# Row maxima transposed in fp32, then split into two bf16 rows on the way out of PSUM

## What is computed

```
attn = einsum('bhqd,bhkd->bhqk', q, k) * scale
attn = softmax(attn)                       # exp(score - row maximum) / sum
y = einsum('bhqk,bhkd->bhqd', attn, v)
```

## Time and profile before

| what | before |
|---|---|
| runs: median (lowest to highest) | 5286.25 us (5284.78 to 5296.24), 3 runs |
| profiled execution: device time | 5298.91 us |
| its span | 5297.2 us |
| PE, DVE, ACT, POOL busy | 93%, 74%, 73%, 38% |
| stage A, first and last row copy | 139.1 to 1118.2 us |
| stage X | 1187.2 to 2217.0 us |
| stage F | 2283.1 to 3630.5 us |

### The profile page before, as it was taken

One profiled execution on the slowest core, in us unless ns is written; L12 is line 12 of the kernel. 1 busy time (PEld: TensorE's weight loads), 2 busy tenths in 40 slices (PEclk: granted clock), 3 DMA queues, 4 the chain that ended last, 5 costly groups with the idle time before them and its releaser, 6 DMA issues. The chain is left out here.

```text
span 5297.2 us, 147856 instructions
## 1 busy us (share of the span) xinstructions
PE 4926.9 (93%) x45659; PEld 4001.1 (76%) x45660; DVE 3899.7 (74%) x9253; ACT 3865.1 (73%) x8215; POOL 2027.2 (38%) x1692
## 2 busy tenths in 40 slices
PE   0999999979999999889999999995799999999998
PEld 0777777758888888667777777773599999899997
DVE  7888888868888888689999999997744444344433
ACT  5899999958888888767777777773655555555554
POOL 1222232313333333234444444442144544444443
PEclk9999999989999999999999999997799999999999
DMA  6777777746666666467777777772432332323222
GB/s 189 184 188 187 190 186 189 187 125 194 196 196 197 196 197 197 138 170 185 186 185 186 183 185 186 185 185 70 52 64 47 63 57 45 64 49 64 47 47 28
DMA packets 631700, 750.63 MB, mean 142 GB/s; under 512 B 143365, under 2 KB 560334, under 8 KB 631472
## 3 DMA queue, kind: packets, MB, share of 16 engines
q1 hardware_dynamic: 575136, 679.62, 49.0%
q0 software_dynamic: 49152, 63.09, 7.3%
q10 hardware_dynamic: 7184, 5.00, 0.3%
HBM read 476.49 MB, written 272.24 MB: 141 GB/s over the span
## 5 line engine op out<-in xcount | busy, mean ns | idle before, releaser
L1762 POOL DMA_INDIRECT out_dram<-exp_gated,exp_token x256 | 419.7, 1639 | 717.6 <-ACT exp_gated L1666 377.1
L1011 DVE TENSOR_REDUCE F_tops<-F_score 128x2 f32<-128x512 f32 x1024 | 668.8, 686 | 22.6 <-PE F_score L706 14.3
L1712 DVE TENSOR_TENSOR exp_hT_lo<-exp_whole,exp_hT_hi 128x512 fp32r<-128x512 f32 x512 | 355.4, 694 | 437.1 <-ACT exp_hT_hi L1655 437.1
L871 ACT ACTIVATE F_probs<-F_scoreT 128x512 f32<-128x512 f32 x1024 | 571.4, 591 | 74.7 <-PE F_scoreT L677 73.4
L1011 DVE TENSOR_REDUCE A_tops<-A_score 128x3 f32<-128x384 f32 x1024 | 526.9, 553 | 83.9 <-PE A_score L696 65.5
L1615 PE MATMUL exp_res<-exp_w_hi,exp_hT_hi 128*128 128x256 f32 x2048 | 573.5, 280 | 0.0
L1617 PE MATMUL exp_res<-exp_w_lo,exp_hT_hi 128*128 128x256 f32 x2048 | 568.0, 277 | 0.0
L1618 PE MATMUL exp_res<-exp_w_hi,exp_hT_lo 128*128 128x256 f32 x2048 | 567.9, 277 | 0.0
L1666 ACT ACTIVATE exp_gated<-exp_y,exp_gate 128x256 f32<-128x256 f32 x256 | 109.4, 498 | 624.1 <-DVE exp_y L1736 594.5
L871 ACT ACTIVATE A_probs<-A_scoreT 128x384 f32<-128x384 f32 x1024 | 463.3, 481 | 17.2 <-PE A_scoreT L665 8.8
L1602 PE MATMUL exp_hid<-exp_xT_hi,exp_w_lo 128*128 128x512 f32 x1024 | 405.9, 396 | 0.0
(11 more groups left out here) (355 smaller groups left out, 14326.1 us busy)
## 6 DMA issues: line engine op xcount, KB each, us to landing
QS<-d_q SPq DMA_DIRECT2D x384, 192.0 KB, 3.7
KS<-d_k SPq DMA_DIRECT2D x256, 192.0 KB, 4.0
QS<-d_q SPq DMA_DIRECT2D x384, 128.0 KB, 3.8
KS<-d_k SPq DMA_DIRECT2D x256, 128.0 KB, 4.0
d_q<-A_q_parts SPq DMA_DIRECT2D x64, 384.0 KB, 3.0
d_k<-A_k_parts SPq DMA_DIRECT2D x64, 384.0 KB, 2.8
QS<-d_q SPq DMA_DIRECT2D x384, 64.0 KB, 3.6
d_q<-X_q_parts SPq DMA_DIRECT2D x64, 384.0 KB, 2.6
```

Source lines behind the costliest of these rows:

```text
L871: nc.scalar.activation(probs[m][0:KR, at:at + HB, :].rearrange("p u x -> p (u x)"), scoreT[i % TB][0:KR, 0:HB * TCOL], ACT.Exp)\
L1011: nc.vector.tensor_reduce(dst, src, AX.X, ALU.max).then_inc(score_read, 1)
L1712: v.tensor_tensor(hT_lo[:, f, :], whole[f % OB][:, :], hT_hi[:, f, :], ALU.subtract).then_inc(h_split, 1)
L1762: nc.gpsimd.indirect_dma_start(out, bass.IndirectOffsetOnAxis(token[j % (2 * XB)][:, s:s + 1], 0), gated[par][:, s, :], None, bounds_check ...
```

## The change

The maxima stay fp32 in the token-major tile and are transposed as fp32. Out of the work bank, ACT copies 16 partitions x 128 into bf16 (`top_rows`), and DVE then subtracts that copy from the same PSUM values into a second bf16 tile (`top_rest`). So DVE has new steps rowsA and rowsB, which wait for ACT's cast (`top_cast`), and it is DVE that marks the bank drained; SP waits for that and sends two DMAs, one for each row. In X and F the reductions write straight into the tile that is transposed, topA and topB are gone, and PE waits for the reads (`score_read`) instead; the reductions write to a tile for each half, and wait ahead of maxima 0 and 8 (in X 0 and 4) until the tile was transposed. In A topA and topB are two fp32 operations, a copy and a maximum. In DVE's list of A, rowsB stands behind maxima 2 and rowsA behind maxima 9; in X rowsB behind maxima 0 and rowsA behind proj; in F rowsB behind maxima 2 and rowsA behind proj.

```diff
@@ -317,8 +317,8 @@
               "maxima attend maxima rowsA attend attend maxima attend attend maxima maxima"),
         "ACT": ("q_rest k_rest evac1 attend attend rowsB seed attend attend xT attend seed attend q attend seed "
               "attend k attend attend seed attend attend rowsA attend seed attend attend evac0 attend"),
-        "DVE": ("topB maxima v maxima maxima maxima maxima maxima maxima tok0 maxima maxima topA tok1 maxima "
-              "maxima maxima maxima norm maxima maxima maxima"),
+        "DVE": ("topB maxima v maxima maxima rowsB maxima maxima maxima maxima tok0 maxima maxima topA tok1 maxima "
+              "rowsA maxima maxima maxima norm maxima maxima maxima"),
         "POOL": ("k_rest q_rest k q"),
     },
     "X": {
@@ -327,8 +327,8 @@
               "q maxima wo attend k maxima attend proj rowsA pv0 maxima attend attend maxima"),
         "ACT": ("seed k_rest seed seed evac1 q_rest rowsB attend seed attend xT0 ctxT aT xT1 attend yT seed seed "
               "q attend attend attend seed k rowsA seed evac0 attend attend"),
-        "DVE": ("topB v mcopy maxima tok0 tok1 norm maxima maxima maxima maxima topA wo stats maxima var c0 c1 "
-              "proj c2 c3 c4 c5 maxima c6 c7 c8 maxima c9 c10 apply"),
+        "DVE": ("v mcopy maxima rowsB tok0 tok1 norm maxima maxima maxima maxima wo stats maxima var c0 c1 "
+              "proj rowsA c2 c3 c4 c5 maxima c6 c7 c8 maxima c9 c10 apply"),
         "POOL": ("k_rest q_rest fetch q refetch k"),
     },
     "F": {
@@ -339,8 +339,8 @@
               "attend"),
         "ACT": ("attend attend attend evac1 attend rowsB attend attend k_rest xT attend aT q attend attend q_rest "
               "attend h2T attend rowsA route attend evac0 attend attend k attend attend xw"),
-        "DVE": ("topB maxima v maxima maxima tok0 tok1 maxima maxima maxima maxima maxima topA stats var maxima "
-              "maxima proj ustats uvar maxima c0 c1 maxima c2 c3 c4 maxima c5 route c6 c7 maxima c8 c9 maxima "
+        "DVE": ("maxima v maxima maxima rowsB tok0 tok1 maxima maxima maxima maxima maxima stats var maxima "
+              "maxima proj rowsA ustats uvar maxima c0 c1 maxima c2 c3 c4 maxima c5 route c6 c7 maxima c8 c9 maxima "
               "c10 maxima apply uapply"),
         "POOL": ("k_rest refetch q q_rest uapply k"),
     },
@@ -415,7 +415,7 @@
     NU = len(UNITS)
     assert NU % 2 == 0
 
-    LINKS = {"topA": 3 if kind == "A" else 2, "topB": 3 if kind == "A" else 2, "norm": {"A": 2, "X": 1, "F": 0}[kind], "stats": 1, "var": 1, "ustats": 1, "uvar": 1, "tok0": 1, "tok1": 3 if kind == "A" else 1}
+    LINKS = {"topA": 2, "topB": 2, "norm": {"A": 2, "X": 1, "F": 0}[kind], "stats": 1, "var": 1, "ustats": 1, "uvar": 1, "tok0": 1, "tok1": 3 if kind == "A" else 1}
     LINKS.update({c: 1 for c in NEWTON_OPS})
 
     def turns(b, name):
@@ -441,6 +441,12 @@
         return base % 2, NU // 2 * b + base // 2
 
     ORDER = [n for n, _ in STEPS["DVE"] if n in LINKS]
+    CASTS = [n for n, _ in STEPS["ACT"] if n in ("rowsA", "rowsB")]
+
+    def counted(g, name):
+
+        b = g - LAG[name]
+        return total(b, [(n, 1) for n in CASTS]) + sum(present(b, n) for n in CASTS[:CASTS.index(name)]) + 1
 
     def linked(g, name):
 
@@ -480,10 +486,12 @@
         probs = [sb(f"probs{i}", [P, H // 2, TCOL]) for i in range(2)]
         outT = sb("outT", [P, 4, 256])
         tok, rec = sb("tok", [P, 2, 256]), sb("rec", [P, 2, H])
-        tops = sb("tops", [P, 3, H])
-        top_wide = [sb(f"top_parts{i}", [P, P], BF16) for i in range(2)]
-        top_parts = [t[:, 0:2 * H].rearrange("p (a h j) -> p a h j", a=2, j=2) for t in top_wide]
-        top_rows = [sb(f"top_rows{i}", [2 * H, P], BF16) for i in range(2)]
+        top_wide = [sb(f"tops{i}", [P, P]) for i in range(2)]
+        tops = [t[:, 0:H].rearrange("p (h n) -> p n h", n=2) for t in top_wide]
+        if kind == "A":
+            thirds = [sb(f"thirds{i}", [P, 3, H // 2]) for i in range(2)]
+        top_rows, top_rest = ([sb(f"{n}{i}", [H, P], BF16) for i in range(2)] for n in ("top_rows", "top_rest"))
+        top_cast = sem("top_cast")
         xdt = BF16 if kind == "A" else F32
         xin, grid = sb("xin", [P, 2, 256]), sb("grid", [P, 2, 256])
         xw, xT = sb("xw", [P, 2, 256], xdt), [sb(f"xT{i}", [P, 2, 256], xdt) for i in range(2)]
@@ -610,11 +618,11 @@
                         if name in ("rowsA", "rowsB"):
                             h = "AB".index(name[4])
                             drained(g, name)
-                            sp.dma_start(QS[gp][96:98, H // 2 * h:H // 2 * (h + 1), :], top_rows[h][:, :])\
-                                .then_inc(rows_in[h], 16)
+                            for row, src in ((96, top_rows), (97, top_rest)):
+                                sp.dma_start(QS[gp][row:row + 1, H // 2 * h:H // 2 * (h + 1), :], src[h][:, :]).then_inc(rows_in[h], 16)
                 sp.wait_ge(result_out, 16 * B)
                 for h in range(2):
-                    sp.wait_ge(rows_in[h], 16 * B)
+                    sp.wait_ge(rows_in[h], 32 * B)
                 if kind == "F":
                     sp.wait_ge(h2_out, 16 * B)
                 if kind == "X":
@@ -651,7 +659,7 @@
                         if name == "attend":
                             s = scoreT[i % TB]
                             if i % (G // 2) == 0:
-                                pe.wait_ge(rows_in[i // (G // 2)], 16 * g + 16)
+                                pe.wait_ge(rows_in[i // (G // 2)], 32 * g + 32)
                             if i == 0 and kind == "X":
                                 pe.wait_ge(maskT_ready, g + 1)
                             need(pe, probs_full, earlier(g, i, TB))
@@ -806,9 +814,12 @@
                                         last = mm(W[:, j * 256:(j + 1) * 256], xT[gp][:, c, j * P:(j + 1) * P], wv[:, c, :],
                                                   start=c == 0, stop=c == 1)
                         elif name in ("rowsA", "rowsB"):
-                            top = "top" + name[4]
-                            pe.wait_ge(link_v, linked(g, top) + LINKS[top])
-                            last = nc.tensor.transpose(Wb[:, 0:P], top_wide["AB".index(name[4])][:, :], ident_b[:, :])
+                            top, h = "top" + name[4], "AB".index(name[4])
+                            if kind == "A":
+                                pe.wait_ge(link_v, linked(g, top) + LINKS[top])
+                            else:
+                                pe.wait_ge(score_read, G * g + G // 2 * (h + 1))
+                            last = nc.tensor.transpose(W[:, 0:P], top_wide[h][:, :], ident_f[:, :])
                         elif name in ("tok0", "tok1"):
                             j = int(name[3])
                             pe.wait_ge(outs_read, 2 * g + 2)
@@ -946,8 +957,9 @@
                                     last = nc.scalar.activation(dst[:, m, 0:n], src, ACT.Identity, bias=bias, scale=scale)
                         elif name in ("rowsA", "rowsB"):
                             h = "AB".index(name[4])
-                            need(act, rows_in[h], 16 * g)
-                            last = nc.scalar.activation(top_rows[h][:, :], Wb[0:2 * H, 0:P], ACT.Copy)
+                            need(act, rows_in[h], 32 * g)
+                            nc.scalar.activation(top_rows[h][:, :], W[0:H, 0:P], ACT.Copy).then_inc(top_cast, 1)
+                            continue
                         elif name == "aT":
                             drained(g - 1, "proj")
                             last = nc.scalar.activation(aT[:, :, :], W[:, :].rearrange("p (c t) -> p c t", c=2), ACT.Copy)
@@ -1003,11 +1015,14 @@
                             chain = Chain(dve, link_v, linked(g, name), LINKS[name], C["passed"])
                         if name == "maxima":
                             dve.wait_ge(score_full, G * g + i + 1)
+                            h, at = divmod(HB * i, H // 2)
+                            if at == 0 and kind != "A":
+                                drained(g - 1, "rows" + "AB"[h])
                             if kind == "A":
-                                src, dst = score[i % SB][:, 0:384].rearrange("p (n k) -> p n k", n=3), tops[:, 0:3, i]
+                                src, dst = score[i % SB][:, 0:384].rearrange("p (n k) -> p n k", n=3), thirds[h][:, 0:3, at]
                             else:
                                 src = score[i % SB][:, 0:2 * HB * KN].rearrange("p (u n k) -> p u n k", u=HB, n=2)
-                                dst = tops[:, 0:2, HB * i:HB * i + HB].rearrange("p n u -> p u n")
+                                dst = tops[h][:, 0:2, at:at + HB].rearrange("p n u -> p u n")
                             nc.vector.tensor_reduce(dst, src, AX.X, ALU.max).then_inc(score_read, 1)
                         if name == "mcopy":
                             dve.wait_ge(mask_in, 16 * g + 16)
@@ -1016,14 +1031,15 @@
```

(13 more changed lines are left out.)

## The result

The changed kernel takes **5478.94 us** (median of 4 runs, 5472.45 to 5479.15) against 5287.09 in the runs beside it: a ratio of 1.036 (95% interval 1.034 to 1.037), 3.6% slower, where 5438 was forecast.

The account below looks back on a forecast made before the run. No engine has much room, so waits decide: A turns on ScalarE, F and X on TensorE. A 89, F 51 and X 12 sum to 152 us on 5298.9, giving 5451, less 12.7: median 5438 us, range 5340 to 5515.

Parts of the forecast that it names:

- the offset: Profiled execution of the kernel before stood 12.7 us over the runs' median; the sum 5451 became a forecast median of 5438.
- F's upper ends: Stage F, highest losses an iteration: 1.4 us for rowsA if uvar again takes 0.89, 0.3 for rowsB.
- The new wait in A: Stage A, rowsA: VectorE stands 1.5 us for ScalarE's cast, ScalarE stalls 1.54; net +1.44 us an iteration, +89 us.
- rowsA in F: Stage F, behind proj: VectorE stands some 2.8 us for the cast; TensorE's maxima 13 waits some 0.65 us an iteration.
- rival (2): Heavier: uvar stays held in F (44 us) and SP's queue binds in X (25 us more): 5507 us; chance 0.14.
- rowsB in F: Stage F: TensorE's tok1 waits for the work bank until the subtraction drains it; 0.17 us an iteration, ends 0 and 0.3.
- X: Stage X: V starts earlier without topB, tok1 waits for the subtraction, fp32 transpose adds 0.05; +0.2 us an iteration, +12 us.
- The failed step: SyncE's queue in X: second DMAs add 1.0 us an iteration against 0.8 waiting for ScalarE, 0.2 over; taken as within X's price.
- The subtraction: VectorE's new 16 x 128 subtraction out of PSUM: 0.29 us by interpolation, never held by GpSimd; if held, 5506 us.
- VectorE's relief: X and F: two small VectorE operations a half removed, one of 1.28 us in F; priced at nothing.

Follow-up runs that it names:

- e1: Changed kernel with rowsA moved behind maxima 12 instead of maxima 9 in VectorE's list of stage A alone; 5387.05 us, ratio 1.018.
- e7: Changed kernel with rowsA moved behind maxima 10 instead of maxima 9 in VectorE's list of stage A alone; 5429.03 us, ratio 1.026.
- e2: Changed kernel with rowsA moved behind c1 instead of proj in VectorE's list of stage F alone; 5437.03 us, ratio 1.028.
- e6: Changed kernel with rowsA behind maxima 12 in A and c1 in F, and F's tok1 behind the next maxima on TensorE and VectorE; 5330.03 us, ratio 1.007.
- e4: Changed kernel with one DMA a rows step instead of two; the subtraction is made but its result not sent; 5464.13 us, ratio 1.032.
- e5: Kernel before with the rows sent by two DMAs of 16 partitions instead of one of 32; 5313.29 us, ratio 1.004.
- e8: Changed kernel, X alone: a VectorE copy doubles the maxima columns, one operation makes both rows, one DMA sends them; 5478.97 us, ratio 1.035.
- e12: Kernel before with norm moved behind maxima 9 instead of maxima 12 in VectorE's list of stage A; 5586.85 us, ratio 1.056.

## Why the prediction was right in its direction and 41 us low

Of the 41 us, 12.7 are the offset: the profiled execution of before stood 12.7 above the median and that of the changed kernel, at its own median, doesn't. The stages make the rest: 152 forecast, 187 measured, 7 given back elsewhere. One sum of the range is off: F's upper ends, 1.4 and 0.3, make 105 us and not 99, so the high ends together are 253; the range that was given doesn't hang on it.

- **The new wait in A: right.** Forecast 1.5 us of standing on VectorE, a stall of 1.54 on ACT and +1.44 an iteration; measured 1.68, 1.32 and +1.4 (16.8 for 15.4) in five iterations of six. e1 and e7 show that it is the place, carried over one to one. **Missing**: the lowered clock, 16 to 17 us. It was no term and no rival.
- **rowsA in F: right.** 2.8 forecast and 2.90 measured; uvar 0.18 and 0.17; 0.65 for the place and 0.68 by e2. uvar wasn't held, so the first part of rival (2) is out.
- **rowsB in F: too small.** Forecast 0.17; e2 leaves 20 us, 0.31. tok1 waits 0.32, and moving it gives 0.11 back (e6). Another part is rowsA's fp32 transpose, 0.10 where 0.05 was taken; TensorE is busy 1000.00 of 1000 in the kernel before, so no wait of its own takes that up.
- **X: near in size by luck, wrong in cause.** Forecast +12 from tok1 and V; measured +19, and it is SP's second issue: without it 16 of the 19 are gone (e4), and alone it costs 22 (e5). The failed step is "it comes out 0.2 over, no more than X is priced at anyway". The issues were sized well (0.5 a step forecast, 0.43 measured), but 0.86 against 1.0 us of idle time was already too much (e5). The wait at tok1 came, and in e4 it cost nothing; that topB's removal pays for it is likely (e8 against e4) and not shown by itself. Two parts of rival (2) thus split: SP binds, uvar doesn't hold.
- **The subtraction: right.** 0.29 by interpolation, 0.28 measured, never held.
- **VectorE's relief: right at nothing, net.** DVE is busy 168 us less in 1000 of F (778.88 against 946.79 in the earlier trace rows), 17.4 us a steady iteration for 20.2. More than half of that isn't work that went: in e2, with the same instructions as the changed kernel, it is 19.0 (876.58 in the same 1000), since the operations that POOL holds are long again. And no stage is shorter than before in any form of the change, not even where the waits are moved away (e6).

## What to carry to other kernels

A step that takes its input from two engines in turn (transpose, cast, subtract) belongs in the in-order list of the third behind the moment when the input is ready, not behind where its operands were made; read that moment off the other engines' timelines, and move work that doesn't need it in front. One word moved in each of two lists was worth 134 us here (92 and 42), while a VectorE busy for 67% of the span in place of 74% showed no gain. And an issuing queue's idle time is no reserve: ask what is issued behind the new DMA and who waits for it.

## What the hardware showed that was not expected

- A stall of TensorE of a microsecond can cost more than its length. The granted clock fell from 1.00 to 0.50 at the end of the idle stretch, for 3.4 us in one iteration of six of the changed A and for some 7 us in each iteration of e12, where a delay of 2.8 us made the iteration about 4.7 us longer ((1276.1-979.1)/63.5). With a stall of 1.3 us (e7) it never fell in A.
- A DMA issue costs SyncE nearly as much for 16 partitions as for 32: 0.55 and 0.60 against 0.72 us. Two halves cost 0.43 more than the whole.
- What one fp32 transpose of 128 columns costs over a bf16 one depends on the matmul behind it. From its start to the next matmul's (medians, kernel before and changed kernel): 0.16 and 0.26 us ahead of the router's in F, 0.06 and 0.11 ahead of a score matmul (rowsB in A and in X), 0.19 and 0.19 ahead of an attend (rowsB in F).
- The length of a small VectorE operation can depend on its moment alone: 0.17 or 0.89 us for the same variance, 0.72 or 1.89 for the same pair of operations in A. The variance ends with POOL's operation each time that it is long.
